# Weight loads issued behind the first group's four transpositions, and a rewritten order of the first steps, in an attention + mixture kernel on one core

## The reference

```python
q = h @ Wq.T; k = h @ Wk.T; v = h @ Wv.T + bv          # h = layernorm(x)
scores = q k^T * 384 ** -0.5 + (adj + adj)              # per head
p = softmax(scores); x = x + (p @ v) @ Wo.T + bo
```

## Time and profile before

| | us |
|---|---|
| median of 3 runs | 2169.67 (2169.14 to 2174.21) |
| the profiled execution, its own time | 2163.93 |
| its span in the profile | 2162.1 |
| PE busy | 2041.2 (94%) |
| DVE busy | 1733.2 (80%) |
| ACT busy | 1629.0 (75%) |
| POOL busy | 1599.6 (74%) |

### The profile page before, as it was taken

The page is one execution under the profiler, slowest core; times in us unless marked ns, Lnnn a source line. Parts: engine busy times, 40 slices in busy tenths (PEclk is TensorE's granted clock), DMA queues, the critical chain, the costliest instruction groups (busy, mean ns, idle before and its releaser), DMA issues.

```text
span 2162.1 us, 54120 instructions
## 1 busy us (share of the span) xinstructions
PE 2041.2 (94%) x16813; PEld 1234.6 (57%) x16813; DVE 1733.2 (80%) x6572; ACT 1629.0 (75%) x5618; POOL 1599.6 (74%) x2418
## 2 busy tenths in 40 slices
PE   4389999999999999999999999999999999999998
PEld 2245555566555566655566655556665556665555
DVE  3968878888888888887888887888887888887884
ACT  3557788777778777778877788877777877778884
POOL 1577777877787777778787777787778777777783
PEclk7689999999999999999999999999999999999999
DMA  5356675656765666666566676566666566667651
GB/s 170 74 113 121 134 135 123 123 124 130 129 140 125 124 128 125 133 137 127 124 125 122 127 137 133 123 122 126 129 129 138 124 127 122 127 139 126 125 91 52
DMA packets 651647, 269.41 MB, mean 125 GB/s; under 512 B 526176, under 2 KB 650720, under 8 KB 651360
## 3 DMA queue, kind: packets, MB, share of 16 engines
q1 hardware_dynamic: 647712, 264.52, 60.5%
q10 hardware_dynamic: 3648, 1.43, 0.3%
HBM read 39.33 MB, written 25.17 MB: 30 GB/s over the span
## 4 chain that ended last, share of the span: by engine, by line
PE 40%; SPq 20%; DVE 9%; ACT 9%; DMA 8%; POOL 8%; issue 6%; ACTq 0%; DVEq 0%; POOLq 0%
SPq L555 19%; PE B_bank L579 18%; PE A_bank L579 14%; DMA PT<-P_parts 3%; ACT S L813 3%; DMA Ks<-k_hi 3%; DVE S L1094 2%; POOL S L1281 2%; PE A_bank L670 2%; PE A_bank L649 2%; DMA h1T<-h_parts 2%; ACT P_parts L742 2%; PE B_bank L678 1%; POOL P_parts L1268 1%; ACT q_hi L786 1%
## 5 line engine op out<-in xcount | busy, mean ns | idle before, releaser
L813 ACT ACTIVATE S<-S,smin 128x128 f32<-128x128 f32 x1536 | 593.4, 391 | 43.2 <-DVE smax L1100 43.2
L1094 DVE CUSTOM_DVE_ANT_0 S<-A_bank,adj,s_unit 128x128 f32<-128x128 f32 x1536 | 434.1, 346 | 104.1 <-POOL P_parts L1268 74.1
L1268 POOL TENSOR_TENSOR P_parts<-S,P_parts 128x512 f16<-128x512 f32 x384 | 442.6, 1161 | 72.9 <-ACT P_parts L742 72.5
L1281 POOL TENSOR_TENSOR S<-S,rowf 128x512 f32<-128x512 f32 x384 | 390.2, 1044 | 10.0
L742 ACT ACTIVATE P_parts<-S 128x512 f16<-128x512 f32 x384 | 237.0, 625 | 129.8 <-DMA PT<-P_parts 90.3
L813 ACT ACTIVATION_READ_ACCUMULATOR S<-S,smin 128x1 f32 x1536 | 293.8, 191 | 0.0
L1100 DVE TENSOR_REDUCE smax<-S 128x12 f32<-128x1536 f32 x128 | 222.1, 1735 | 2.1
L579 PE MATMUL A_bank<-wv_hi,h1T 128*128 128x384 f16 x768 | 209.9, 329 | 0.0
L649 PE MATMUL A_bank<-Ks,Qs 96*128 96x128 f16 x1536 | 139.0, 222 | 52.5 <-DMA Ks<-k_hi 33.7
L579 PE MATMUL A_bank<-h1T,wq_hi 128*128 128x512 f16 x576 | 175.9, 388 | 3.2 <-DMA h1T<-h_parts 1.8
L579 PE MATMUL A_bank<-h1T,wk_hi 128*128 128x512 f16 x576 | 172.1, 380 | 0.0
(11 more groups left out here) (204 smaller groups left out, 5763.2 us busy)
## 6 DMA issues: line engine op xcount, KB each, us to landing
xin<-in_x SPq DMA_DIRECT2D x32, 768.0 KB, 4.5
Qs<-q_hi SPq DMA_DIRECT2D x256, 96.0 KB
out<-x SPq DMA_DIRECT2D x128, 192.0 KB, 2.2
Ks<-k_hi SPq DMA_DIRECT2D x252, 96.0 KB, 2.2
Qs<-q_lo SPq DMA_DIRECT2D x128, 96.0 KB
Ks<-k_lo SPq DMA_DIRECT2D x126, 96.0 KB, 2.2
adj<-in_adj SPq DMA_DIRECT2D x32, 256.0 KB, 3.1
PT<-P_parts SPq DMA_TRANSPOSE x384, 3.3
```

What stands on the lines that cost most here:

```text
L813: ins = nc.scalar.activation(S[b % 2][:, h, :], S[b % 2][:, h, :], ACT.Exp, bias=smin[b % 2][:, h:h + 1], scale=-1.0, accum_out=ssum[b % 2 ...
L1094: ins = nc.vector.tensor_tensor_reduce(S[b % 2][:, h, :], src[:, j * T:(j + 1) * T], adj2[:, b, :], s_unit[:], 3.0e38, ALU.add, ALU.min, s ...
L1268: nc.gpsimd.tensor_tensor(P_parts[:, c, 1, :], S[b % 2][:, c * HPC:(c + 1) * HPC, :].rearrange("p j k -> p (j k)"), P_parts[:, c, 0, :], A ...
L1281: nc.gpsimd.tensor_tensor(S[b % 2][:, hs, :], S[b % 2][:, hs, :], rowf[b % 2][:, hs].unsqueeze(2).broadcast_to([P, HPC, T]), ALU.mult).the ...
```

## The change

SP issues first x of group 0, wq, wk, wv and five rows, then its step list. Right behind the fourth transposition of group 0 it issues the rest (`late_loads`): wv2 and wg1 (no longer issued by ACT), the two halves of wqk from index 4 and 5 of the list, adj, x of group 1, wo and wp. The first scale now covers three weights (wq, wk, wv), the second three, so the counts that PE and ACT wait for change. The opening's step lists are rewritten for all five queues. Of these moves the text below uses: on DVE `A.ln1@1` stands ahead of `W.lo.0`, `W.rowbias` stands behind `A.qk.2@1` and ahead of `A.qk.3@1` where it stood ahead of `A.norm.2@0`, and `W.bias` stands ahead of `A.score.3.0@0` where it stood ahead of `A.score.2.0@0`; on POOL `A.norm.2@0` is followed by one turn, vl.2, `W.lo.6`, one turn, `W.lo.7`; on ACT the weight highs follow all four transposed inputs.

```diff
     "act": """
-        A.h1.0@0 A.hT.0@0 A.h1.1@0 A.hT.1@0 A.h1.2@0 W.hi.0@0 A.hT.2@0 A.h1.3@0 A.hT.3@0 W.sum.5@0 W.sum.4@0
+        A.h1.0@0 A.hT.0@0 A.h1.1@0 A.hT.1@0 A.h1.2@0 A.hT.2@0 A.h1.3@0 A.hT.3@0 W.hi.0@0 W.hi.1@0 W.sum.5@0
...
     "dve": """
-        A.ln1@0 W.max.0@0 W.max.1@0 W.top.0@0 W.scale.0@0 W.max.2@0 W.lo.0@0 W.unit.0@0 W.max.7@0 W.top.1@0
-        W.lo.1@0 A.ln1@1 W.scale.1@0 A.qk.0@0 A.qk.1@0 A.qk.2@0 W.unit.1@0 A.qk.3@0 W.lo.2@0 A.qk.4@0 A.qk.5@0
-        W.top.2@0 W.scale.2@0 W.values.0@0 A.v.0@0 A.v.1@0 A.score.0.0@0 A.score.0.1@0 A.score.0.2@0 A.smax.0@0
-        W.unit.2@0 A.v.2@0 A.score.1.0@0 A.score.1.1@0 A.score.1.2@0 A.norm.0@0 A.smax.1@0 W.lo.3@0 A.v.3@0
-        W.bias.0@0 A.score.2.0@0 A.score.2.1@0 A.score.2.2@0 A.norm.1@0 A.smax.2@0 W.rowbias.0@0 A.norm.2@0
-        A.score.3.0@0 A.score.3.1@0 A.score.3.2@0 A.qk.0@1 A.qk.1@1 A.mix.0@0 A.qk.2@1 A.smax.3@0 A.qk.3@1
-        A.qk.4@1 A.mix.1@0 A.qk.5@1 A.proj.0@0 A.proj.1@0 A.ln2.0@0
+        A.ln1@0 W.max.0@0 W.max.1@0 W.max.2@0 W.top.0@0 W.scale.0@0 A.ln1@1 W.lo.0@0 W.lo.1@0 A.qk.0@0
+        W.unit.0@0 W.lo.2@0 A.qk.1@0 A.qk.2@0 W.max.7@0 W.top.1@0 A.qk.3@0 A.qk.4@0 A.qk.5@0 W.top.2@0
+        W.scale.1@0 W.unit.1@0 W.values.0@0 W.scale.2@0 A.v.0@0 A.v.1@0 A.score.0.0@0 A.score.0.1@0
+        A.score.0.2@0 A.smax.0@0 A.score.1.0@0 A.score.1.1@0 A.score.1.2@0 A.smax.1@0 A.norm.0@0 A.v.2@0 A.v.3@0
+        W.lo.3@0 W.unit.2@0 A.score.2.0@0 A.score.2.1@0 A.score.2.2@0 A.norm.1@0 A.smax.2@0 W.bias.0@0
+        A.score.3.0@0 A.score.3.1@0 A.norm.2@0 A.score.3.2@0 A.smax.3@0 A.qk.0@1 A.mix.0@0 A.qk.1@1 A.qk.2@1
+        W.rowbias.0@0 A.qk.3@1 A.qk.4@1 A.qk.5@1 A.proj.0@0 A.mix.1@0 A.ln2.0@0 A.proj.1@0
     """,
...
-        A.turn.1.0@0 A.turn.1.1@0 A.turn.1.2@0 A.norm.2@0 A.turn.2.0@0 A.turn.2.1@0 A.vl.2@0 W.lo.6@0 W.lo.7@0
+        A.turn.1.0@0 A.turn.1.1@0 A.turn.1.2@0 A.norm.2@0 A.turn.2.0@0 A.vl.2@0 W.lo.6@0 A.turn.2.1@0 W.lo.7@0
...
-        scale_part = (slice(0, 2), slice(2, 6), slice(6, 8))
+        scale_part = (slice(0, 3), slice(3, 6), slice(6, 8))
...
-            for n in range(2):
+            for n in range(3):
                 load_raw(n)
-            sp.dma_start(rows[1][1], rows[1][0].unsqueeze(0).broadcast_to([P, C])).then_inc(bo_loaded, 16)
-            sp.dma_start(xin[1][:], dram_group(x, 1)).then_inc(x_loaded[1], 16)
-            load_raw(2)
-            sp.dma_start(adj2[:], dram_group(adj, 0)).then_inc(adj_loaded, 16)
-            for n in (3, 4, 5, 6):
-                load_raw(n)
-            for src, dst in rows[:1] + rows[2:5]:
-                sp.dma_start(dst, src.unsqueeze(0).broadcast_to([P, dst.shape[1]])).then_inc(consts_loaded, 16)
+            for n, (src, dst) in enumerate(rows[:5]):
+                sp.dma_start(dst, src.unsqueeze(0).broadcast_to([P, dst.shape[1]]))\
+                    .then_inc(bo_loaded if n == 1 else consts_loaded, 16)
+
+            def late_loads():
+                sp.dma_start(staged(V2, VG)[:, :, 0:C], wv2).then_inc(raw_loaded[7], 16)
+                sp.dma_start(staged(V2, VG)[:, :, C:VG], wg1).then_inc(raw_loaded[7], 16)
+                for n in (4, 5):
+                    load_raw(n)
+                sp.dma_start(adj2[:], dram_group(adj, 0)).then_inc(adj_loaded, 16)
+                sp.dma_start(xin[1][:], dram_group(x, 1)).then_inc(x_loaded[1], 16)
+                for n in (3, 6):
+                    load_raw(n)
...
                         .then_inc(h1_turned[b % 2], 16)
+                    if g == 0 and b == GB - 1:
+                        late_loads()
...
-                        pe.wait_ge(maxima, (2, 4, 4)[b])
+                        pe.wait_ge(maxima, (3, 4, 4)[b])
                         if b > 0:
                             pe.wait_ge(sums, 2 * b)
+                            pe.wait_ge(tops, b)
...
                         pe.wait_ge(tops, b + 1)
+                        if b > 0:
+                            pe.wait_ge(wscale_ready, b)
...
-                act.wait_ge(wscale_ready, (1, 1, 2, 2, 2, 2, 3, 3)[col])
+                act.wait_ge(wscale_ready, (1, 1, 1, 2, 2, 2, 3, 3)[col])
...
-            act.dma_start(staged(V2, VG)[:, :, 0:C], wv2).then_inc(raw_loaded[7], 16)
-            act.dma_start(staged(V2, VG)[:, :, C:VG], wg1).then_inc(raw_loaded[7], 16)
```

More of the change, by code:

```diff
@@ L89 @@
     "pe": """
[L90 to L93, removed]
+        W.warm.1@0 W.turn.0@0 W.spread.0@0 A.qk.0@0 A.qk.1@0 A.qk.2@0 A.qk.3@0 A.qk.4@0 W.turn.1@0 A.qk.5@0
+        W.turn.2@0 W.spread.1@0 A.v.0@0 A.v.1@0 W.spread.2@0 A.score.0.0@0 A.score.0.1@0 A.score.0.2@0
+        A.score.1.0@0 A.v.2@0 A.score.1.1@0 A.score.1.2@0 A.v.3@0 A.score.2.0@0 W.warm.0@0 A.score.2.1@0
+        A.score.2.2@0 A.score.3.0@0 A.score.3.1@0 A.score.3.2@0 A.qk.0@1 A.mix.0@0 A.qk.1@1 A.qk.2@1 A.qk.3@1
         A.qk.4@1 A.mix.1@0 A.qk.5@1 A.proj.0@0 A.proj.1@0
@@ L96 @@
     "act": """
-        A.h1.0@0 A.hT.0@0 A.h1.1@0 A.hT.1@0 A.h1.2@0 W.hi.0@0 A.hT.2@0 A.h1.3@0 A.hT.3@0 W.sum.5@0 W.sum.4@0
[L98 to L101, removed]
+        A.h1.0@0 A.hT.0@0 A.h1.1@0 A.hT.1@0 A.h1.2@0 A.hT.2@0 A.h1.3@0 A.hT.3@0 W.hi.0@0 W.hi.1@0 W.sum.5@0
+        A.h1.0@1 W.sum.4@0 A.qk.0@0 W.hi.2@0 A.qk.1@0 W.sum.3@0 A.qk.2@0 W.sum.6@0 A.qk.3@0 A.hT.0@1 A.qk.4@0
+        A.h1.1@1 A.hT.1@1 A.qk.5@0 W.stack.1@0 A.v.0@0 W.hi.3@0 A.v.1@0 W.hi.4@0 W.hi.5@0 W.hi.6@0 A.h1.2@1
+        A.score.0.0@0 A.score.0.1@0 A.score.0.2@0 A.score.1.0@0 A.score.1.1@0 A.turn.0.0@0 A.turn.0.1@0 A.h1.3@1
+        A.turn.0.2@0 A.hT.2@1 A.score.1.2@0 A.hT.3@1 W.hi.7@0 A.turn.1.0@0 A.score.2.0@0 A.turn.1.1@0
         A.score.2.1@0 A.turn.1.2@0 A.score.2.2@0
@@ L104 @@
     "dve": """
-        A.ln1@0 W.max.0@0 W.max.1@0 W.top.0@0 W.scale.0@0 W.max.2@0 W.lo.0@0 W.unit.0@0 W.max.7@0 W.top.1@0
-        W.lo.1@0 A.ln1@1 W.scale.1@0 A.qk.0@0 A.qk.1@0 A.qk.2@0 W.unit.1@0 A.qk.3@0 W.lo.2@0 A.qk.4@0 A.qk.5@0
-        W.top.2@0 W.scale.2@0 W.values.0@0 A.v.0@0 A.v.1@0 A.score.0.0@0 A.score.0.1@0 A.score.0.2@0 A.smax.0@0
-        W.unit.2@0 A.v.2@0 A.score.1.0@0 A.score.1.1@0 A.score.1.2@0 A.norm.0@0 A.smax.1@0 W.lo.3@0 A.v.3@0
-        W.bias.0@0 A.score.2.0@0 A.score.2.1@0 A.score.2.2@0 A.norm.1@0 A.smax.2@0 W.rowbias.0@0 A.norm.2@0
-        A.score.3.0@0 A.score.3.1@0 A.score.3.2@0 A.qk.0@1 A.qk.1@1 A.mix.0@0 A.qk.2@1 A.smax.3@0 A.qk.3@1
-        A.qk.4@1 A.mix.1@0 A.qk.5@1 A.proj.0@0 A.proj.1@0 A.ln2.0@0
+        A.ln1@0 W.max.0@0 W.max.1@0 W.max.2@0 W.top.0@0 W.scale.0@0 A.ln1@1 W.lo.0@0 W.lo.1@0 A.qk.0@0
[5 more added lines that the diff above has]
+        W.rowbias.0@0 A.qk.3@1 A.qk.4@1 A.qk.5@1 A.proj.0@0 A.mix.1@0 A.ln2.0@0 A.proj.1@0
     """,
     "pool": """
-        A.ln1@0 A.hT.0@0 A.hT.1@0 A.hT.2@0 A.hT.3@0 A.ln1@1 W.adj.0@0 A.hT.0@1 W.lo.4@0 A.vl.0@0 W.lo.5@0
-        A.vl.1@0 A.hT.1@1 A.norm.0@0 A.turn.0.0@0 A.turn.0.1@0 A.turn.0.2@0 A.hT.2@1 A.hT.3@1 A.norm.1@0
-        A.turn.1.0@0 A.turn.1.1@0 A.turn.1.2@0 A.norm.2@0 A.turn.2.0@0 A.turn.2.1@0 A.vl.2@0 W.lo.6@0 W.lo.7@0
+        A.ln1@0 A.hT.0@0 A.hT.1@0 A.hT.2@0 A.hT.3@0 A.ln1@1 W.adj.0@0 A.hT.0@1 A.hT.1@1 A.vl.0@0 A.vl.1@0
+        W.lo.4@0 W.lo.5@0 A.norm.0@0 A.turn.0.0@0 A.turn.0.1@0 A.turn.0.2@0 A.hT.2@1 A.hT.3@1 A.norm.1@0
+        A.turn.1.0@0 A.turn.1.1@0 A.turn.1.2@0 A.norm.2@0 A.turn.2.0@0 A.vl.2@0 W.lo.6@0 A.turn.2.1@0 W.lo.7@0
     """,
@@ L119 @@
         A.hT.0@0 A.hT.1@0 A.hT.2@0 A.hT.3@0 A.stack.0@0 A.stack.1@0 A.hT.0@1 A.hT.1@1 A.turn.0.0@0 A.turn.0.1@0
-        A.hT.2@1 A.hT.3@1 A.turn.0.2@0 A.turn.1.0@0 A.turn.1.1@0 A.turn.1.2@0 A.adj@0 A.turn.2.0@0 A.stack.0@1
+        A.hT.2@1 A.turn.0.2@0 A.hT.3@1 A.turn.1.0@0 A.turn.1.1@0 A.adj@0 A.turn.1.2@0 A.turn.2.0@0 A.stack.0@1
         A.stack.1@1 A.turn.2.1@0 A.turn.2.2@0 A.turn.3.0@0 A.turn.3.1@0 A.turn.3.2@0
```

## The result

The changed kernel takes 2174.1 us, the median of 12 runs (2170.6 to 2178.28), beside 2168.63 for the kernel before (12 runs, 2164.52 to 2174.21): a ratio of 1.0021 with an interval of 1.0013 to 1.003. It is slower by 5.5 us, where 4.7 us less were forecast, and outside the range. The same kernel on another chip gave 1.0045 [1.0027, 1.0062], 11.4 us above before, so the size of the loss is known only to some 6 us, though its sign is clear in both.

The account below looks back on a forecast made before the run. PE paces an untouched steady state, so only the start of group 1's scores counts: 2.7 us from earlier loads plus 2.0 from the new order make 4.7, giving 2165.0 us against the 2169.67 median, range 2158 to 2172.

Parts of the forecast that it names:

- The marks: Starts of the first scores (62.24 us before) and group 1's scores (129.54); what the second gains, the end gains.
- Ready does not mean landed: SP's queue serves in order, so the first transposition lands behind weights and five rows: at 18.1 us.
- the worst bound: First transposition's landing if five rows cost 1.87 us each, as bo_row did: rows end at 20.5, it lands at 21.2.
- the middle: First transposition's landing taken between 15.0 and 21.2 us, at 18.1, since neither row price was nearer.
- the floor: First transposition limited only by its own issue and landing: 12.1 + 2.9 = 15.0 us.
- first product right behind the low half of wq: Sign of being right: PE's first q product starts right behind that DVE step, near 35 us.
- Part 2: Order behind the first scores: bias-row chain, slowed beside POOL, ends at 115.0; group 1's scores start 2.0 us earlier.
- Rival (b): Late x is late by its issue, 12.6 us ahead of it; first product at 40.8, total 2173.3; chance 0.10.
- Rival (c): An opening chain unseen between 130 and 210 us absorbs the gain: no change, 2169.7; chance 0.13.
- Rival (a): Rows land fast or the lock costs little: 5.8 + 4.1 = 9.9 us gained, 2159.8; chance 0.35.

Follow-up runs that it names:

- quiet front: Changed kernel with group 1's x ahead of the transpositions, bias rows on ACT's queue, gate loads last on SP, ACT's weight sums later: 2156.26 us, 0.9963 of before.
- rows last: Changed kernel with the five bias rows issued behind all late loads instead of ahead of the transpositions: 2164.57 us, 0.9997 of before.
- x first: Changed kernel with x of group 1 issued first of the late loads: 2163.29 us, 0.9989 of before.

## Why the prediction was wrong

The marks were the right ones. From group 1's scores to the end of the span the profiles of the eleven edited kernels have 2030.8 to 2036.3 us, before has 2032.6, and the two profiles of the changed kernel itself 2038.5 and 2038.9; so the total goes with the mark within some 6 us. These are single executions, whose times spread by as much. The mark was to be at 129.54 - 4.7 = 124.8 and came at 136.1, 11.3 later. The steps:

1. **What holds the transposition, mis-sized: 6.8 us.** The step "Ready does not mean landed" was right as a mechanism, and its value, 18.1, was not: 24.9, beyond the worst bound of 21.2. Three kernels divide it: the transposition lands at 15.2 with neither the rows nor the gate's loads in flight, at 18.9 with the gate's loads alone, at 24.9 with both. So the rows are worth 6.0 here, nearly the 6.2 of the worst bound (21.2 - 15.0); the middle gave them 3.1. The gate's loads, 3.7, stood at nothing: the bound took the queue of SP alone, though `bg_row` takes 18.5 us from issue to landing in the profile of before too. 2.9 + 3.7 + 0.2 for the floor is the 6.8. The 3.7 rests on the quiet front, which differs in more than these loads. The worst bound also counted five full rows where one of the five has 16 KB; landing to landing they took 23.9 - 10.95 = 12.9.
2. **The late loads, mis-sized: 3.3 us.** From the landing 13.2 us were given to x, 16.5 were needed (24.9 to 41.4). The issue of the transpositions took the 4.2 foreseen. The rest, 9.0 in the sum (1.5 until the transpositions end and 7.5 for 2800 KB at the full queue's 373 GB/s), took 12.3, from 29.1 to 41.4, or 228 KB a us. The queue ran at 35 to 308 GB/s from 30 to 36 us and passed 350 only from 36. With x issued first, 4.0 of its 6.1 us were lost in the same way, and here 4.8 of 12.3, so most of the loss lies in the start of the stretch and not in its bytes. A rate read where a queue has been full for long is not the rate of a stretch that starts from empty.
3. **From x to the first product: right.** 3.8 us, as forecast; the forecast "first product right behind the low half of wq" is the row at 45.27. The text gave that place in DVE's list a price of 11 us (23.9 for 35.1); measured at the product it is 14.7, since x was later still.
4. **From the product to the first scores: 0.8 more** (25.2 against 24.4). Nothing shortened, as said; the first products ran at half pace for 6.2 us (45.27 to 51.45) where before has 4.9 (37.81 to 42.75).
5. **Part 2: right within 0.3 us, and by its mechanism.** 65.6 us from the first scores to the second, before 67.3: a gain of 1.7 for 2.0. The bias chain took 17.3 instead of 15.0, but it also began 35.7 us behind the first scores instead of 37.8, and the two hang together: the forecast let one operation through for each POOL instruction, and eight for seven were held, each until a POOL instruction ended. POOL's last turn ended 47.1 us behind the first scores (117.65; forecast 46.8), and the 14 operations left took 5.8 (forecast 6.0 for 15). So the chain's end follows POOL's, and an earlier start only puts more of the chain beside it.

The terms 6.8 + 3.3 + 0.8 + 0.3 = 11.2 make up the difference. Rival (b), the only one slower than before, named the late x and a first product at 40.8, but its reason is false: the six late loads up to x were issued in 3.9 us (29.08 to 32.97), 0.5 to 0.7 each, and not in 12.6. It decided "once x lands after 36", and that condition came true by landing instead. A landing bound of my own, 21.2, and 4.2 for the issue, plus the 217 KB a us of wv (12.9 us for 2800 KB), would have put x at 38 and the product at 42, and the forecast on the slow side; I used the slow rate for wv and the fast one for x without a reason.

Rival (c), an opening that is absorbed, fell with the sign of the result: 6.6 us at the mark are 5.5 in the medians (11.4 on the other chip), and the two kernels whose mark is 10.4 and 11.3 us ahead of before's are 7.1 and 13.9 us faster than the before timed beside them. Rival (a), the rows at the full queue's rate or a lock that costs little, was the side on which most of the remaining chance lay; the rows went the other way, and the chain took 17.3 us.

## What to carry to other kernels

Before loads are put ahead of a step, add up what every queue has in flight there, the small ones of other issuing engines too, and price them at the rate of a comparable stretch, its start included. When a load is made late, look for the step that consumes it in each engine's fixed order: here one input of the next group held the weights' low half of the first behind it, and moving either the load (one line, 6.9 us at the mark) or the step (11.4 us) was worth more than the change could have brought. Such prices do not add in full: rows last, x first and the step's place together gave 17.9 at the mark where their sum would be 24.5. Two of them act on the same wait for x.
